# A graph network on one core: the node features are loaded when the last tile of the count matrix begins, and the square root's table is loaded right behind the square

## What is computed

```python
edge_index = jnp.stack([src, dst])
h = jnp.maximum(_layernorm(x, axis=-1), 0.0)
x = x + _L0_gnn_ref(h, edge_attr_16, src, dst, ...)   # two rounds of messages and a GRU
h = jnp.maximum(_layernorm(x, axis=-1), 0.0)
x = x + _L1_gnn_ref(h, edge_index, ...)               # two graph convolutions
h = jnp.maximum(_layernorm(x, axis=-1), 0.0)
x = x + _L2_gnn_ref(h, edge_index, edge_attr_16, ...) # mean over neighbours
h = jnp.maximum(_layernorm(x, axis=-1), 0.0)
x = x + _L3_gnn_ref(h, edge_index, edge_attr_32, ...) # an edge network and a GRU
```

## Time and profile before

| | us |
|---|---|
| median of 3 runs | 4882.58 (4882.41 to 4883.76) |
| the profiled execution's own time | 4881.64 |
| its span in the trace | 4879.8 |
| DVE busy | 2846.7 (58%) |
| PE busy | 3312.7 (68%) |
| POOL busy | 2046.2 (42%) |

### The profile page before, as it was taken

One profiled execution on the slowest core, in us unless ns is written; L12 is line 12 of the kernel. 1 busy time (PEld: TensorE's weight loads), 2 busy tenths in 40 slices (PEclk: granted clock), 3 DMA queues, 4 the chain that ended last, 5 costly groups with the idle time before them and its releaser, 6 DMA issues. The chain is left out here.

```text
span 4879.8 us, 93316 instructions
## 1 busy us (share of the span) xinstructions
PE 3312.7 (68%) x24444; PEld 2509.9 (51%) x24445; DVE 2846.7 (58%) x7446; ACT 886.2 (18%) x1811; POOL 2046.2 (42%) x2644
## 2 busy tenths in 40 slices
PE   3332577787769899899989644555555556666666
PEld 2222233333349789798989533343444444444445
DVE  6667788777765534312323355555666666666775
ACT  1221123566630112100011100000000000000002
POOL 4666400000000211111111377777777777777770
PEclk6555899888889999999999655555555555555558
DMA  3000000111135234354544222222333233333330
GB/s 143 0 0 1 10 21 40 56 56 59 59 117 199 84 122 162 126 176 159 185 146 158 71 64 64 67 69 67 69 72 72 72 72 74 74 76 74 77 76 20
DMA packets 173539, 403.74 MB, mean 83 GB/s; under 512 B 47902, under 2 KB 109481, under 8 KB 172809
## 3 DMA queue, kind: packets, MB, share of 16 engines
q1 hardware_dynamic: 52409, 259.35, 14.9%
q10 hardware_dynamic: 69360, 91.59, 6.7%
q0 software_dynamic: 51680, 51.82, 6.0%
HBM read 359.52 MB, written 43.07 MB: 83 GB/s over the span
## 5 line engine op out<-in xcount | busy, mean ns | idle before, releaser
L704 POOL DMA_INDIRECT scr<-ptable,src_i x1566 | 1522.4, 972 | 481.5 <-issue 398.3
L673 POOL COPY late<-late 128x256 f32<-128x256 f32 (+1 forms) x65 | 25.9, 398 | 1950.8 <-POOLq L671 1950.8
L1037 PE MATMUL ps_front<-scr,arena 128*128 128x192 bf16 x7203 | 612.2, 248 | 66.7 <-PEq L1035 66.7
L1146 PE MATMUL ps_front<-stat_w,scr 128*128 128x392 fp8e4 x2064 | 492.7, 368 | 234.3 <-PEq L1150 206.9
L1037 PEld LDWEIGHTS ps_front<-scr,arena 128*128 128x128 fp8e4 x7203 | 601.2, 99 | 76.3 <-issue 74.5
L907 ACT ACTIVATE arena<-arena 128x384 f32<-128x384 f32 x309 | 161.6, 523 | 1859.6 <-ACTq L906 1859.6
L959 PE MATMUL ps_front<-arena 128*128 (+1 forms) x930 | 176.5, 362 | 436.0 <-PEq L957 436.0
L1658 DVE TENSOR_TENSOR scr<-scr,late 128x384 bf16<-128x384 f16 x1024 | 364.1, 356 | 183.6 <-DVEq L1657 175.7
L959 PE MATMUL ps_back<-arena 128*128 x924 | 175.4, 362 | 399.1 <-PEq L957 399.1
L1146 PEld LDWEIGHTS ps_front<-stat_w,scr 128*128 128x128 bf16 x2064 | 186.3, 104 | 503.5 <-issue 465.3
L1037 PE MATMUL ps_front<-arena 128*128 128x192 bf16 x4802 | 406.0, 248 | 23.4 <-PEq L1035 23.4
(11 more groups left out here) (342 smaller groups left out, 4782.4 us busy)
## 6 DMA issues: line engine op xcount, KB each, us to landing
arena<-a_dram SPq DMA_DIRECT2D x245, 784.0 KB, 4.4
arena<-low_dram ACTq DMA_DIRECT2D x309, 192.0 KB, 3.3
a_dram<-arena SPq DMA_DIRECT2D x49, 784.0 KB, 3.3
arena<-in_e32g ACTq DMA_DIRECT2D x309, 96.0 KB, 3.2
scr<-ptable,src_i POOLq DMA_INDIRECT x1566
arena<-in_e16p SPq DMA_DIRECT2D x1, 13387.5 KB, 35.6
x<-in_x_nm SPq DMA_DIRECT2D x1, 1664.0 KB, 8.1
out_nm<-x SPq DMA_DIRECT2D x1, 1664.0 KB
```

The costliest lines, as they stand in the source:

```text
L704: pool.indirect_dma_start(grow[:, g % RING, j, :], None, ptable, bass.IndirectOffsetOnAxis(ap=src_i[:, g * GC + j:g * GC + j + 1], axis=0) ...
L1037: last = pe.matmul(ps_z[b % 2][:, 0:3 * H], amat[b][:, i, :], hsp[k % 2][:, i, :], start=(i == 0), stop=(i == NT - 1))
L1146: return pe.matmul(bank_w[i][:, 0:WC], oh_lo[u][:, j, :], oh_hi[u][:, j, :], **{"start": False, "stop": False, **flags})
```

## The change

The load of x moves in SP's queue: it now stands behind the loop over the first 48 tiles and ahead of the last tile's store, and waits for a new semaphore `s_xf`. DVE raises it in the last tile, directly behind `load_runs`. For that DVE's last tile is taken out of the loop and stands as code of its own (`build_tile(NT - 1)`). On ACT, `norm()` loads the root's table directly behind the square.

```diff
@@ semaphores
+        s_xf = sem("s_xf")
@@ SP
                 stored(0)
                 stored(1)
+            sp.wait_ge(s_xf, 1)
+            sp.sem_inc(s_xf, -1)
+            sp.dma_start(x[:, :, :], D["x_nm"].rearrange("p (t f) -> p t f", f=H)).then_inc(s_x, 16)
             store(NT - 1, 0)
             stored(0)
             sp.dma_start(low_i, D["dst_lin"].rearrange("(p k) -> p k", p=P)).then_inc(s_dl, 16)
-            sp.dma_start(x[:, :, :], D["x_nm"].rearrange("p (t f) -> p t f", f=H)).then_inc(s_x, 16)
@@ ACT, norm
                 act.activation(pair[:, :, 0:H], pair[:, :, H:], ACT.Square).then_inc(s_sqd, 1)
+                act.preload_act_table(ACT.Sqrt)
                 act.wait_ge(s_sq, 1)
@@ DVE, build_tile
+                last = isinstance(t, int)
...
                         runs = load_runs(v, win_tab[0:1, ds(t, 1), 0, :, :].rearrange("o t a w -> o (t a w)"),
                                          (CH - 1, GWMAX - 1))
+                        if last:
+                            v.sem_inc(s_xf, 1)
@@ DVE, behind the tables
-            with v.Fori(DENSE, NT) as t:
+            with v.Fori(DENSE, NT - 1) as t:
                 build_tile(t)
+            build_tile(NT - 1)
```

## The result

The changed kernel takes 4867.63 us (median of 7 executions, 4866.15 to 4869.7), beside 4883.11 us (4882.41 to 4885.47, 7 executions) for the kernel before on the same chip. The ratio is 0.9967 with a 95% interval of 0.9957 to 0.9977. So it is faster by 15.5 us. So it was wrong in size, not in sign. The profiled execution took 4866.15 us.

The account below looks back on a forecast made before the run. The chain from x's load through the norm to PE's first sums was taken to bound the stretch, PE the sums. 9.7 + 1.3 = 11.0 us gained, giving a median of 4871.6 us, range 4869.5 to 4877.0.

Parts of the forecast that it names:

- The load of x: Before DVE's sum over x: issued near 1374.2, landed by 1382.3 (8.1 us), so the 12.0 us wait goes to nothing.
- What is late next: ACT's square then waits for the copies to `auxT`, starting at 1394.1 in place of 1403.83: gain 9.7 us, not 12.
- The table: Root's table load on ACT hides beside DVE's sum of squares: gain 1.3 us.
- the rival of a dear switch: Table switch has a drain that now hides too: 4870.2 us by the page, 4871.0 from rows; chance 0.05.
- The last tile's own code: DVE's last tile as straight, unseen code: cost taken as 0, up to 3.9 us at the other end.
- 3.9 us stall: Rival: DVE's last tile waits for its code, gain 7.1, 4875.5 us; chance 0.22, of which 0.04 for twice.
- PE's clock: At the first sums: low clock for 3.0 us costs about 1.5; left unchanged, effect -1.5 to +1.5 us.
- The failed step: After the first sums: no later stage keeps its own time, so the edit's worth is how far PE's start moves.
- The place of later code: Rival: new code shifts DVE's later loops, 3.9 us per jump back, 300 us in the edge network, 5172 us; chance 0.04.

Follow-up runs that it names:

- e8: Changed kernel with ACT's square put ahead of the last three copies to `auxT`: 4866.37 us, ratio 0.9964 to the kernel before.
- e2: Kernel before with only the early load of the square root's table added: 4883.95 us, ratio 0.9999.
- e14: Changed kernel without the early load of the square root's table, DVE code the same: 4868.09 us, ratio 0.9968 to the kernel before.
- e4: Changed kernel with DVE's last tile kept in the loop, the semaphore raised in each of 45 plain tiles: 4873.99 us, ratio 0.998 to the kernel before.
- e13: Changed kernel with 2 short extra operations (writing zeros) in DVE's norm: 4878.63 us, ratio 0.9988 to the kernel before.
- e3: Kernel before with only DVE's last tile taken out of the loop as its own code: 4883.89 us, ratio 1.0001.
- e1: Kernel before run once more, unchanged, for scatter: 4883.97 us, ratio 1.0001.
- e6: Changed kernel with 4 short extra operations (writing zeros) in DVE's norm: 4877.89 us, ratio 0.9986 to the kernel before.
- e7: Changed kernel with 8 short extra operations (writing zeros) in DVE's norm: 4875.87 us, ratio 0.9983 to the kernel before.

## Why the prediction was wrong, step by step

**The load of x:** right. The wait is gone. x landed sooner than assumed, in 7.1 us.

**What is late next:** right. The copies to `auxT` held the square. From aux to the square is 21.50 us before and 11.67 after: 9.83 where the sum has 9.7. e8 confirms the cause, since moving the square ahead of three copies frees another 2.3 us.

**The table:** right up to the first sums (aux to root shrinks by 11.10, so 1.27 beside the square's 9.83), and no drain, so the rival of a dear switch is out. The Trainium skill (ScalarE: Activation LUTs, "What ACT_TABLE_LOAD costs") has 2.66 us for it; here it is the 1.28 of its row. But as a term of the time it was wrong: of its 1.3 us the traces of e2 and e14 have 0.1 left at the fourth pass.

**The last tile's own code:** right where it runs. Its first window comes behind 2.19 us of idleness (the earlier trace rows has 2.70 before), and instructions were fetched in 2 packets between 1366 and 1384:

```profile
q14 instruction: 2, 0.02, 0.4%
```

No 3.9 us stall came, so that rival fell. The Trainium skill (Runtime: NRT & Kernel Launch, "Instruction fetch mechanics") says that code is fetched in order, ahead of its use, and these rows agree.

**PE's clock:** the cause of the miss, with the step after it. The prediction weighed it only at the first sums, with 1.5 us either way. Of the 11.1 us freed 10.2 are left at s4. By the traces' records of the granted clock, PE runs 4.0 us at the low level at the start of the first pass (1417.97 to 1422) in place of 3.0, 5.9 in place of 5.2 at the second, and 5.6 in place of 5.4 at the third. At half speed that is 0.9 us, the whole of the loss. e8 freed 13.4 and kept all of it. The larger effect lies at the fifth pass, where 4.1 us came back. The low stretch there and the late fall of the clock make up about 4.0 of them, by the same estimate as for e4.

**The failed step** is this sentence: "There is nothing later that keeps a time of its own", and with it "whatever moves PE's start moves all that follows". PE's granted clock keeps its own time in each later stage. An offset of about a microsecond was swallowed by it (e2, e13, e14 up to s4), and one of 0.6 us that passed a point at the fifth pass (e13) was paid with 4 us more. That a rise of the clock need not move with PE's start is shown; what sets the place of a rise is not. The prediction looked for a wait of an engine and did not ask this of the clock, though the earlier trace rows show it rising in the midst of a stage.

**The place of later code** was named as a rival, but only as a loss, and by the price of a fetch, 3.9 us at each jump. Shown is 0.10 us at each jump, with the sign of a gain: 1.0 us in the second convolution. It matters beyond its size, for without it PE reaches s5 at about 1083.3 us behind aux, as in e4, and the 4.1 us don't come. That fits with neither part alone having the surplus: e3 arrives at 1095.42, far from the point, and e4 just behind it.

In the profiled spans the sum reads: 1.3 from the build's end (scatter), 11.1 up to the first sums, -0.9 by the clock, 1.0 from the loop, 4.1 by the clock in the last layers, -1.2 behind the gather: 15.4. For the medians e4 stands for the edits of the norm with 10.6, and the changed kernel's two measurements add 4.2 and 4.9 to it.

**What stays open.** Which places of the code are good for the loop, and why. What sets the point at the fifth pass. And "gather to end" scatters from 2109.9 to 2120.2 between traces. The same program has 2109.89 and 2113.27 (before, e1). e6 and e13 have 2119.54 and 2120.16, and gained 1 to 2 us less than e7 though less delay was put in. Four of the microseconds that they lose on the changed kernel are at the fifth pass; what else is gone lies mostly in the edge network, and no run tells why. Their moved code might do it, which was not tested; the trace of e2, with the DVE code of before, also has 2118.8, so it can happen without.

## What to carry to other kernels

A wait that is removed is worth what the next one leaves, and that can be read from the trace to a tenth of a microsecond; what the end of a long program makes of it can't, where the granted clock changes between stages. Before an offset of a few microseconds is carried to the end, look at every later stage that starts with a low clock: it may swallow the offset or give several times as much. And an edit that makes an engine's code longer moves its later loops, so compare it with a kernel that has the same waits and the old length. This holds for experiments too: a delay made of added instructions tests two things at once.

## What the hardware showed that was not expected

- The rise of PE's granted clock did not follow PE's start: 0.81 us between two starts, both at 0.50 up to 1422 and at 1.00 from there. A delay of 0.89 us at the first sums was 0.01 at the fourth pass.
- A start of the fifth pass 1.1 us earlier gave a clock that rose near 2466 in place of 2470 and was still at 1.00 at 2716 to 2718 where the other had 0.50: 4.5 us in one stage (289.8 against 294.3).
- Eight rounds of the same loop took 136.87, 137.70 or 138.63 us by the place of its code alone. Behind the loop the same operations took 8.23 or 8.86 us.
- An added delay of 1.28 us that moved no DVE code cost nothing (e14). One of 0.9 us that moved it by 4 instructions came with 8.0 us less of the gain (e13), and one of 3.5 us that moved it by 16 with 6.9 us less (e7).
